# Flamingo block with experts, one core: value sums in SBUF, sixteen ScalarE copies for the attended rows, and a new order in the first part

## The reference, cut to what matters

```
x = x + tanh(g_xattn[0]) * L0_xattn(layernorm(x), ctx)   # stage 1
x = x + tanh(g_ffn[0])   * L0_ffn(layernorm(x))          # stage 2
x = x + tanh(g_xattn[1]) * L1_xattn(ctx, ctx, layernorm(x))
x = x + tanh(g_ffn[1])   * L1_ffn(layernorm(x))
```

```
qk   = einsum('blih,bljh->blij', Q, K) / sqrt(16)
attn = softmax(qk, axis=-1)
valued = einsum('blij,bljh->blih', attn, V)
return valued.swapaxes(-2, -1).reshape(b, length, d) @ Wo.T
```

## Time and profile before

| what | value |
|---|---|
| median of 3 runs | 764.0 us (761.69 to 764.12) |
| profiled execution | 763.81 us, of which its span 762.0 |
| mean granted TensorE clock | 0.98 |
| PE busy | 693.1 us, 91% |
| DVE busy | 633.2 us, 83% |
| POOL busy | 422.1 us, 55% |
| ACT busy | 392.3 us, 51% |

### The profile page before, as it was taken

The page is one execution under the profiler, slowest core; times in us unless marked ns, Lnnn a source line. Parts: engine busy times, 40 slices in busy tenths (PEclk is TensorE's granted clock), DMA queues, the critical chain, the costliest instruction groups (busy, mean ns, idle before and its releaser), DMA issues.

```text
span 762.0 us, 12814 instructions
## 1 busy us (share of the span) xinstructions
PE 693.1 (91%) x4381; PEld 591.8 (78%) x4381; DVE 633.2 (83%) x927; ACT 392.3 (51%) x699; POOL 422.1 (55%) x304
## 2 busy tenths in 40 slices
PE   6749999999999989889999999999976999999996
PEld 4428878787878778657788888888865999989986
DVE  3889999999999964789999999999887777678653
ACT  2313443344343421247777777777743565555643
POOL 3788888888888881413998666667032111110000
PEclk9958999999999999989999999999999999999999
DMA  9501010011118012140544426100010101000000
GB/s 274 215 15 42 29 28 28 28 28 34 49 40 348 8 62 70 31 172 16 199 157 180 182 91 249 29 28 22 15 35 28 39 19 56 29 28 8 16 15 21
DMA packets 28642, 56.43 MB, mean 74 GB/s; under 512 B 3408, under 2 KB 24656, under 8 KB 27440
## 3 DMA queue, kind: packets, MB, share of 16 engines
q1 hardware_dynamic: 23408, 47.64, 17.6%
q0 software_dynamic: 1872, 5.11, 2.4%
q10 hardware_dynamic: 3312, 3.02, 1.2%
HBM read 48.55 MB, written 7.21 MB: 73 GB/s over the span
## 4 chain that ended last, share of the span: by engine, by line
PE 49%; DVE 19%; POOL 12%; issue 10%; ACT 7%; DMA 2%; DVEq 0%; SPq 0%; POOLq 0%; ACTq 0%
PE bank L747 19%; PE bank L738 16%; PE bank L999 9%; POOL PRODV L624 8%; PE bank L755 4%; DVE PRODQ L1562 2%; POOL PRODV L626 2%; DVE SLOT_r L1950 2%; DVE bank L1571 2%; DVE PRODV_r L1950 2%; DVE bank L1652 2%; DVE STC L2038 1%; ACT L1468 1%; ACT XS L1468 1%; ACT L1288 1%
## 5 line engine op out<-in xcount | busy, mean ns | idle before, releaser
L624 POOL TENSOR_TENSOR PRODV<-SHARED 128x2048 f32<-128x2048 f32 x32 | 144.7, 4522 | 30.4 <-DVE bank L1652 25.0
L738 PE MATMUL bank<-ROWS,SLOT 128*128 128x128 f32 x1024 | 122.9, 279 | 0.0
L738 PEld LDWEIGHTS bank<-ROWS,SLOT 128*128 128x128 f32 x1024 | 120.5, 195 | 0.8
L717 POOL TENSOR_TENSOR RS<-VE,MHALF 128x2 f32<-128x2 f32 x16 | 13.1, 819 | 149.3 <-DVE VE L2045 149.3
L626 POOL TENSOR_TENSOR PRODV<-PRODV 128x1024 f32<-128x1024 f32 x32 | 74.7, 2336 | 2.5
L1571 DVE TENSOR_REDUCE bank<-PRODQ 128x256 f32<-128x4096 f32 x16 | 70.7, 4419 | 0.1
L1562 DVE TENSOR_TENSOR PRODQ<-bank,SHARED 128x4096 f32<-128x4096 f32 x16 | 70.6, 4413 | 0.0
L1950 DVE TENSOR_TENSOR PRODQ_r<-SLOT,ROWS_r 128x1024 fp32r<-128x1024 f32 x44 | 63.5, 1472 | 0.8 <-ACT ROWS_r L1375 0.6
L641 POOL DMA_INDIRECT XS<-normal_rows,INV x23 | 26.8, 1164 | 64.5 <-PE bank L755 42.8
L738 PE MATMUL bank<-SLOT,HA 128*128 128x256 f32 x256 | 58.3, 381 | 2.4 <-DVE HA L1760 2.4
L1950 DVE TENSOR_TENSOR W_r<-SLOT,PRODQ_r 128x1024 fp32r<-128x1024 f32 x44 | 58.6, 1332 | 1.7 <-ACT PRODQ_r L1342 1.7
(11 more groups left out here) (275 smaller groups left out, 1912.1 us busy)
## 6 DMA issues: line engine op xcount, KB each, us to landing
SLOT<-wexp SPq DMA_DIRECT2D x9, 3072.0 KB, 11.6
ROWS<-xT SPq DMA_DIRECT2D x16, 128.0 KB, 2.3
SHARED<-ctxT SPq DMA_DIRECT2D x16, 128.0 KB, 2.3
X<-x SPq DMA_DIRECT2D x16, 128.0 KB, 2.6
normal_rows<-ROWS SPq DMA_DIRECT2D x16, 128.0 KB, 1.7
WET<-ctxT SPq DMA_DIRECT2D x4, 512.0 KB, 7.8
out<-X SPq DMA_DIRECT2D x16, 128.0 KB, 1.7
expert_rows<-YS ACTq DMA_DIRECT2D x12, 128.0 KB, 1.7
```

Of the source, the lines that this page charges most:

```text
L624: gp.tensor_tensor(o, pr, v, ALU.mult).then_inc(s["av_prod"], 1)
L738: last = pe.matmul(dst, lhs(k), rhs(k), start=(k == 0), stop=(k == chunks - 1))
```

## The change

Four things change in the first part; the later parts are the same.

The value sums go to PICK, a tile of 128x256 in SBUF that the routing uses later, and no longer to PSUM. The multiply by RI goes from VectorE to ScalarE, where it is sixteen copies of 16 columns, each with one column of RI as its scale (`weighted`). VectorE's order in a step changes: `add_attended` ahead of the second `mult`, the first value sum ahead of `normal_rows`, the reciprocals last; `normal_rows` is written with another instruction. TensorE's order changes: `up_half(t4, 1)` ahead of `attended`, and `queries` between `normal_rows` and `gate` (in step 1 also behind the pair products). The drain keeps its order on TensorE.

```diff
-        AOP = PB[0][:, D:2 * D]
+        AOP = PICK[:, :]
...
             def step(of):
                 t0, t3, t4 = of(0), of(3), of(4)
+                if t4 is not None:
+                    up_half(t4, 1)
                 if t3 is not None:
                     attended(t3)
                     out_rows(t3)
-                if t4 is not None:
-                    up_half(t4, 1)
...
-                    if not first(t0, 1):
-                        queries(t0)
                     if first(t0, 2) and not first(t0, 1):
                         pair_products()
                 if t4 is not None:
                     down_rows(t4)
                 if t3 is not None:
                     normal_rows(t3)
+                if t0 is not None and not first(t0, 1):
+                    queries(t0)
                 if t3 is not None:
                     gate(t3)
                     up_half(t3, 0)
...
+            def weighted(t3):
+
+                n3 = num(t3)
+                act.wait_ge(s["recip"], n3 + 1)
+                act.wait_ge(s["av_read"], 2 * n3 + 2)
+                if not first(t3, 1):
+                    act.wait_ge(s["aT_done"], n3)
+                for i in range(DK):
+                    last = act.activation(AO[:, i * NH:(i + 1) * NH], AOP[:, i * NH:(i + 1) * NH], ACT.Copy,
+                                          scale=RI[:, i:i + 1])
+                last.then_inc(s["a_ready"], 1)
...
                 if t4 is not None:
                     gelu(t4, 0)
                 if t3 is not None:
+                    weighted(t3)
                     attended(t3)
...
-                dve.tensor_scalar(XH[:, t3[1], :], X[:, n3, :], MV[:, 1, 0:1], MV[:, 1, 3:4],
-                                  ALU.subtract, ALU.mult).then_inc(s["xn2_ready"], 1)
+                dve.scalar_tensor_tensor(XH[:, t3[1], :], X[:, n3, :], MV[:, 1, 0:1], spread(MV[:, 1, 3:4], 1, D),
+                                         ALU.subtract, ALU.mult).then_inc(s["xn2_ready"], 1)
...
             def shares(t2):
 
                 dve.wait_ge(s["sums"], num(t2) + 1)
+                if not first(t2, 1):
+                    dve.wait_ge(s["a_ready"], num(t2))
                 dve.reciprocal(RI[:, :], SM[:, 1, :]).then_inc(s["recip"], 1)
...
-                dve.tensor_tensor(AO[:, :].rearrange("p (i h) -> p i h", i=DK), aov,
-                                  spread(RI[:, :].rearrange("p (i o) -> p i o", o=1), 2, NH),
-                                  ALU.mult).then_inc(s["a_ready"], 1)
+                if not first(t2, 1):
+                    dve.wait_ge(s["a_ready"], num(t2))
...
+                if t3 is not None:
+                    add_attended(t3)
                 if t4 is not None:
                     mult(t4, 1)
-                if t3 is not None:
-                    add_attended(t3)
...
                 if t2 is not None:
-                    exp_sums(t2)
-                    shares(t2)
+                    value_sums(t2, 0)
                 if t3 is not None:
                     normal_rows(t3)
                 if t2 is not None:
-                    attended(t2)
+                    value_sums(t2, 1)
+                    shares(t2)
```

More of the change, by code:

```diff
@@ L1316, in drain @@
                 gelu(a, 0)
+                weighted(b)
                 attended(b)
@@ L1321, in drain @@
                 gelu(b, 0)
+                weighted(c)
                 attended(c)
@@ L1636, in normal_rows, with value_sums @@
                     dve.wait_ge(xh_out[t3[1]], 16 * t3[0])
-                dve.tensor_scalar(XH[:, t3[1], :], X[:, n3, :], MV[:, 1, 0:1], MV[:, 1, 3:4],
-                                  ALU.subtract, ALU.mult).then_inc(s["xn2_ready"], 1)
+                dve.scalar_tensor_tensor(XH[:, t3[1], :], X[:, n3, :], MV[:, 1, 0:1], spread(MV[:, 1, 3:4], 1, D),
+                                         ALU.subtract, ALU.mult).then_inc(s["xn2_ready"], 1)
             def shares(t2):
                 dve.wait_ge(s["sums"], num(t2) + 1)
+                if not first(t2, 1):
+                    dve.wait_ge(s["a_ready"], num(t2))
                 dve.reciprocal(RI[:, :], SM[:, 1, :]).then_inc(s["recip"], 1)
-            def attended(t2):
-                n2 = num(t2)
-                aov = AOP.rearrange("p (i h) -> p i h", i=DK)
+            AOV = AOP.rearrange("p (i h) -> p i h", i=DK)
+            def value_sums(t2, hf):
                 H2 = NH // 2
[L1650 to L1657, removed]
-                if not first(t2, 1):
-                    dve.wait_ge(s["aT_done"], n2)
-                dve.tensor_tensor(AO[:, :].rearrange("p (i h) -> p i h", i=DK), aov,
-                                  spread(RI[:, :].rearrange("p (i o) -> p i o", o=1), 2, NH),
-                                  ALU.mult).then_inc(s["a_ready"], 1)
+                dve.wait_ge(s["av_half"], 2 * num(t2) + hf + 1)
+                if not first(t2, 1):
+                    dve.wait_ge(s["a_ready"], num(t2))
+                dve.tensor_reduce(
+                    AOV[:, :, hf * H2:(hf + 1) * H2],
+                    PRODV[:, :].rearrange("p (f i h j) -> p f i h j", f=2, i=DK, h=H2)
+                    [:, hf, :, :, 0:DK // 2], AX.X, ALU.add).then_inc(s["av_read"], 1)
             def add_shared(t4):
@@ L1687, in step @@
                     row_max(t1)
+                if t0 is not None:
+                    guarded_first(t0)
                 if t3 is not None:
@@ L1691, in step @@
                     shift(t1)
+                if t2 is not None:
+                    exp_sums(t2)
                 if t3 is not None:
                     guarded(t3, 1, "ln2")
-                if t0 is not None:
-                    guarded_first(t0)
                 if t2 is not None:
-                    exp_sums(t2)
-                    shares(t2)
+                    value_sums(t2, 0)
                 if t3 is not None:
@@ L1722, in drain @@
                 mult(a, 1)
-                attended(c)
+                value_sums(c, 0)
+                value_sums(c, 1)
                 add_shared(a)
```

## The result

The changed kernel takes 771.09 us (median of 5 executions, 767.28 to 773.05) against 764.0 before (5 executions, 761.69 to 765.19): a ratio of 1.0065, interval 1.0034 to 1.0097. It is slower: by some 5 us by the ratio, by 7.1 us by the two medians alone (1.0093, inside the interval). It lies outside the predicted range of 758 to 768.5. Two later executions, of 3917.61 us (e7) and 1182.14 us (e9), are in the medians given there and not in the ratios; no trace of them exists.

What follows compares the result with a forecast made beforehand. It took a ring of GpSimd and VectorE (root, normal rows, sum, product; about 16.7 us a step) as the bound, TensorE close at 16.41. Start -1.0, steps -4.9, drain +4.6 gave -1.3: 762.5 us, range 758 to 768.5.

Steps and rivals of the forecast that it cites:

- rival B: In each step GpSimd's product gets in before VectorE's normal rows, which wait out its 4.5 us: 804 us; chance 0.04.
- the ring opens: Loop: with VectorE's sum before the normal rows, GpSimd's product waits only for exp; TensorE becomes the bound, 16.19 a step.
- the three other edits: Sums written to SBUF, the later reciprocal, and L1637 as a scalar_tensor_tensor: priced at nothing, within VectorE's slack.
- The start: Step 1: pair products ahead of TensorE's queries, worth between 0 and 1.8 us; 1.0 us saved was taken.
- The steps: Turn 4 to turn 16 of the normal rows: loop step 16.41 to 16.19, shorter last wait; 4.9 us saved together.
- The two terms behind the 0.22: TensorE's loop step: queries filling the gap before the gate save 0.64; the moved up_half's new wait for gelu costs 0.42.
- The copies: ScalarE's sixteen copies at 0.205 us each, 3.37 us with the tail; hidden in the loop with 0.4 us of cover.
- the threshold: Loop: from 0.23 us a copy, TensorE's turn of the attended rows waits for the copies in every step.
- The drain: Tiles 14 and 15: no second up_half covers the copies, so TensorE waits before both turns; 4.6 us lost.
- D: Rival: the drain costs less or the start gives more, as with an earlier TensorE clock rise; 759 us; chance 0.20.
- A: Rival: the copies are too long for their cover; 768.5 us at 0.25 a copy, 774 at 0.27; chance 0.17.
- C: Rival: TensorE's new wait for gelu is 0.7 us, not 0.42, so steps don't get shorter; 765.4 us; chance 0.09.

Runs made afterwards that it cites:

- e7: e1 plus eight unused identity matmuls on TensorE ahead of each of the drain's two turns of the attended rows; 760.94 us, ratio 0.9944.
- e9: The kernel before with only its first value sum moved ahead of the normal rows, from step 4 on; 762.97 us, ratio 0.9969.
- e1: The changed kernel with VectorE's normal rows ahead of the first value sum again, in step 3 alone; 765.93 us, ratio 1.0013.
- e4: The changed kernel with the normal rows written as a tensor_scalar again, nothing else; 768.13 us, ratio 1.0033.
- e5: e3 with TensorE's queries ahead of the pair products again, in step 1 alone; 758.39 us, ratio 0.9917.
- e6: e3 with TensorE's queries behind the keys' product again in every step but step 1; 764.91 us, ratio 1.0001.
- e8: e3 with eight of ScalarE's sixteen copies cut into two halves of 8 columns, 24 copies in all; 767.48 us, ratio 1.0027.
- e3: The changed kernel with e1's exchange in step 3 and, for tiles 14 and 15, VectorE's multiply instead of the copies; 757.98 us, ratio 0.9901.

## Why the prediction was wrong, by its own steps

**The step that failed: rival B's "so VectorE is there first", and with it the price of nothing for the new place of the normal rows.** The prediction saw that the normal rows would now stand beside GpSimd's 4.5 us product, and dismissed it: "the product waits for the sum just ahead of L1637, so VectorE is there first". That holds where both have been waiting for the sum. In step 3 the sum was done 1.4 us before the root (53.45 against 54.88), and both waited for GpSimd's own root L557: the product was next in GpSimd's list and needed nothing more from VectorE, whose rows needed GpSimd's word. So the releasing engine won by 0.07 us. It was the sum's new place ahead of the rows ("the ring opens") that let this happen, and not the scalar_tensor_tensor among "the three other edits": e1 takes the place back and the rows take 0.49, e4 takes the form back and they still take 4.56. B was priced as an all-or-nothing case (twelve steps, 804 us), and I asked it only of a steady step, when the first step of the pipeline has other last arrivals. Its true size was one collision of 4.2, on the chain, in place of the start's gain (e1). The rule of the Trainium skill that I had cited (SBUF — State Buffer, section "SBUF: two separate sides": whichever of the two starts first gets the shared port pair for its whole instruction) is borne out by 4.69 us beside a product of 4.48; I drew the wrong order from it. For e4's 4.56, with one tensor input, the rule asks for a mode that uses two ports, and no run here shows in which mode that instruction ran.

**The start, -1.0 predicted, +3.35 at turn 4.** Apart from the collision the code is 1.5 to 3.3 earlier than before at turn 4 (72.94, 72.82 and 71.22 against 74.47). The sign was right, but the cause that I priced is not shown to give it: e5, with the old order of step 1, is 2.1 earlier too (72.38). At turn 3, where the pair products should show, the new order is 0.3 to 1.5 earlier than before (54.62, 54.56 and 53.49 against 54.96), e5 0.1. From turn 3 to turn 4, for which I took nothing, it is 17.7 to 18.4 against 19.5 before, and 17.5 in e5. How much the pair products gave is not settled (e5: 0.2 to 1.4 at turn 3).

**The steps, -4.9 predicted, -4.75 measured.** Right, step for step: 16.19 in the loop, the last wait 1.18 where 1.0 was taken. The two terms behind the 0.22 were each 0.1 too small and made that up between them, which is luck (e6).

**The copies, 3.37 predicted for all, 3.27 measured**, their cover 0.4 predicted and 0.56 measured, the threshold nearly right (e8).

**The drain, +4.6 predicted, +7.8 measured: the second step that failed.** The mechanism and its waits were right to 0.1 (e7: 4.65 with the waits filled). The missing term is TensorE's clock: I costed two waits of 2 us as 2 us each, although had shown me the engine at the lower level elsewhere. It came to 3.1 to 3.2.

The sum with what was measured: -1.3 as forecast, 4.35 more in the start, 0.15 more in the steps and 3.2 more in the drain make +6.4, the 6.39 of the first expert turn. Of the rivals, D was wrong for the drain and right for the start but for the collision; A and C did not occur. Neither miss alone would have left the range: the forecast with one collision of 4.2 is 766.7, with the clock's 3.2 it is 765.7, with both 769.9, beyond the 768.5.

## What to carry to other kernels

When an exchange puts a VectorE instruction beside a long GpSimd one, ask for every step, the first ones above all, which of the two has its last condition met first. In the three traces in which GpSimd's own result freed VectorE and GpSimd's next instruction needed nothing more, GpSimd won by 0.07 us, and the short instruction took as long as the long one. A wait that a reordering opens for TensorE may bring slower matmuls behind it, here 1.6 us for each 2.07 of waiting, and belongs in the range; work that is hidden in the loop has to be costed anew in the drain, where its cover is missing. And when a change of several edits comes out slower, most of it may be sound: two local repairs turned +0.65% into -1%.

## What the runs showed of the hardware

- A tensor_scalar with one tensor input was held up by GpSimd's product as well (4.56 us, e4), not only the form with two SBUF inputs; the value sums, which read SBUF once and run beside the same product, were not (1.21 against 1.17 to 1.23 us).
- The held-up instruction doesn't slow the product: 4.48 us beside it, 4.5 elsewhere. Where VectorE was there first (e9, 220.14), the product that started 0.17 behind took 4.61, 0.1 more than usual.
- Two idle times of TensorE of 2.07 us were followed by stretches at the lower clock (0.50 over 280 to 282 us); with eight small matmuls in each they were not (e7). Idle times of 4.24 (the change, 572.90) and 4.10 (e3, 558.60) were followed by 0.67 over 4 us and 0.61 over 2 us. Idle times of 2.23 (e1, 566.15), 2.29 (before, 564.65) and 2.38 (before, 268.64) were followed by 1.00. So 2 us can be enough and need not be; what decides is not shown.
- A ScalarE copy of 8 columns took 289 ns and one of 16 columns 296; back to back they stand 0.20 us apart.
